# DLRM tower on one core: each gather waits for the last but one, in place of a wait behind each fifth

## What is computed

```python
e = jnp.stack([tbl_0[ids[:, 0]], ..., tbl_31[ids[:, 31]]], axis=1)   # (2048, 32, 16)
z = jnp.sum(e[:, row, :] * e[:, col, :], axis=2)                     # all pairs row < col: 496
h = jnp.concatenate([z, dense_ctx], axis=1)                          # 512 wide
h = jnp.maximum(h @ W_top1 + b_top1, 0.0)                            # 512 -> 512
h = jnp.maximum(h @ W_top2 + b_top2, 0.0)                            # 512 -> 256
y = h @ W_top3                                                       # 256 -> 1
```

## Time and profile before

| what | us |
|---|---|
| median of 3 runs | 389.74 |
| lowest and highest | 388.18 and 391.79 |
| span of the profiled execution, first to last instruction | 386.4 |
| around it, to the median | 3.3 |
| busy: TensorE's matmuls | 299.7 |
| busy: VectorE | 248.2 |
| busy: POOL | 228.5 |
| busy: ScalarE | 145.3 |

### The profile page before, as it was taken

One profiled execution on the slowest core, in us unless ns is written; L12 is line 12 of the kernel. 1 busy time (PEld: TensorE's weight loads), 2 busy tenths in 40 slices (PEclk: granted clock), 3 DMA queues, 4 the chain that ended last, 5 costly groups with the idle time before them and its releaser, 6 DMA issues.

```text
span 386.4 us, 7087 instructions
## 1 busy us (share of the span) xinstructions
PE 299.7 (78%) x2572; PEld 267.2 (69%) x2572; DVE 248.2 (64%) x326; ACT 145.3 (38%) x311; POOL 228.5 (59%) x250
## 2 busy tenths in 40 slices
PE   1767799886987967988676887877699786978477
PEld 1356689785887856877665886766598675867366
DVE  7699758675666666493756739464683955557541
ACT  3883543443162525244332424424243441113012
POOL 6456655566566656656665666566556656666700
PEclk9889779998999999989999998999969899899859
DMA  6670020202020202102020110202002000000000
GB/s 141 205 242 7 8 64 8 64 8 65 7 63 5 65 5 49 21 6 63 6 64 5 40 29 6 64 6 65 6 9 60 5 7 5 8 6 8 6 2 3
DMA packets 19036, 14.51 MB, mean 38 GB/s; under 512 B 9727, under 2 KB 16461, under 8 KB 19022
## 3 DMA queue, kind: packets, MB, share of 16 engines
q1 hardware_dynamic: 10284, 11.69, 9.5%
q0 software_dynamic: 7680, 1.98, 5.9%
q10 hardware_dynamic: 1058, 0.66, 0.6%
HBM read 14.24 MB, written 0.08 MB: 37 GB/s over the span
## 4 chain that ended last, share of the span: by engine, by line
issue 33%; POOL 28%; DMA 15%; PE 9%; DVE 6%; another core or an unknown queue 4%; ACT 3%; DVEq 1%; ACTq 0%; POOLq 0%
POOL emb L367 28%; DMA emb<-tbl,idx 15%; DVE emb L470 2%; PE bank L683 2%; DVE prod L489 2%; PE bank L663 2%; PE bank L692 1%; PE bank L645 1%; PE bank L780 1%; DVE prod L498 1%; ACT h1T L888 1%; ACT distance L844 1%; ACT onehot L854 1%; DMA idx<-ids 1%
## 5 line engine op out<-in xcount | busy, mean ns | idle before, releaser
L367 POOL DMA_INDIRECT emb<-tbl,idx x240 | 227.3, 947 | 138.4 <-DMA emb<-tbl,idx 73.4
L489 DVE TENSOR_TENSOR prod<-emb,bank 128x1904 f32<-128x1904 f32 (+5 forms) x51 | 94.5, 1854 | 88.3 <-DMA emb<-tbl,idx 88.3
L663 PE MATMUL bank<-ident,prod 128*128 128x128 f32 x768 | 102.8, 287 | 14.0 <-issue 8.6
L663 PEld LDWEIGHTS bank<-ident,prod 128*128 128x128 f32 x768 | 94.4, 197 | 15.9 <-issue 9.9
L683 PE MATMUL bank<-zT,w_sb 128*128 128x128 f32 x480 | 70.6, 295 | 13.6 <-ACT zT L882 12.9
L645 PE MATMUL bank<-parts,onehot 125*128 125x160 bf16 (+1 forms) x816 | 77.0, 244 | 1.4 <-issue 1.3
L683 PEld LDWEIGHTS bank<-zT,w_sb 128*128 128x128 f32 x480 | 63.6, 207 | 16.7 <-issue 14.9
L645 PEld LDWEIGHTS bank<-parts,onehot 125*128 125x128 bf16 x816 | 66.2, 106 | 12.3 <-issue 4.6
L470 DVE TENSOR_REDUCE emb<-bank 128x480 f32 (+5 forms) x96 | 52.7, 584 | 17.2 <-PE bank L645 8.8
L640 PE MATMUL bank<-far_ten,named_ten 100*128 100x480 bf16 (+1 forms) x64 | 24.8, 388 | 33.1 <-issue 24.5
L888 ACT ACTIVATE h1T<-bank,b_sb 128x128 f32<-128x128 f32 x60 | 21.5, 363 | 65.9 <-PE bank L683 26.5
(11 more groups left out here) (71 smaller groups left out, 126.5 us busy)
## 6 DMA issues: line engine op xcount, KB each, us to landing
gids<-small_ids_f SPq DMA_DIRECT2D x16, 544.0 KB
emb<-tbl,idx POOLq DMA_INDIRECT x240
w_sb<-w SPq DMA_DIRECT2D x1, 1024.0 KB
w_sb<-w SPq DMA_DIRECT2D x1, 512.0 KB
tab<-tbl SPq DMA_DIRECT2D x7, 56.0 KB
tab<-tbl SPq DMA_DIRECT2D x5, 70.0 KB
tab<-tbl ACTq DMA_DIRECT2D x5, 70.0 KB
z_last<-dense SPq DMA_DIRECT2D x16, 8.0 KB
```

The source lines that it names most:

```text
L367: nc.gpsimd.indirect_dma_start(emb[:, t, at:at + D], None, tables[f], bass.IndirectOffsetOnAxis(ap=idx[:, t, f:f + 1], axis=0)).then_inc(d ...
L489: return nc.vector.tensor_tensor(prod[:, at * D:(at + n * a) * D].rearrange("p (j i d) -> p j i d", j=n, d=D), strided(emb_at(t, PLACES[g] ...
L663: mm = nc.tensor.matmul(bank[:, Z_BANK + place, c * P:(c + 1) * P], v[:, d, :], ident[:], start=(d == 0), stop=(d == D - 1), is_transpose= ...
```

## The change

`RUN` and its waits go, and so do POOL's waits on `made`, the six semaphores `landed[g][..]` and the five `last_landed`. In their place stand two semaphores, `landed[0]` and `landed[1]`, which the gathers of the whole kernel use in turn, and each gather waits until the last but one has landed (`AHEAD = 2`). VectorE waits for a group, or for a piece of tile 15, by waiting for the last two gathers of it, one on each semaphore.

```diff
@@ constants
+L = len(LARGE)
...
-RUN = 5
+AHEAD = 2
@@ semaphores
-        landed = [[sem(f"landed{g}_{i}") for i in range(2)] for g in range(len(GROUPS))]
-        last_landed = [sem(f"last_landed{i}") for i in range(len(LAST_PIECES))]
+        landed = [sem(f"landed{i}") for i in range(AHEAD)]
@@ POOL
                 for g, n in enumerate(GROUPS):
-                    if t >= 2:
-
-                        pool.wait_ge(made, steps_done(t - 2, GROUP_STEPS[g]))
                     for i in range(n):
+                        gather = t * L + GROUP_AT[g] - S + i
+                        if gather >= AHEAD:
+
+                            pool.wait_ge(landed[gather % AHEAD], 16 * (gather // AHEAD))
                         f = FIELDS[GROUP_AT[g] + i]
                         at = (PLACES[g] + i) * D
-                        done = landed[g][t % 2]
-                        if t == LAST_TILE:
-                            for k, (group, first, count) in enumerate(LAST_PIECES):
-                                if group == g and first <= i < first + count:
-                                    done = last_landed[k]
                         nc.gpsimd.indirect_dma_start(
                             emb[:, t, at:at + D], None, tables[f],
                             bass.IndirectOffsetOnAxis(ap=idx[:, t, f:f + 1], axis=0)
-                        ).then_inc(done, 16)
-                        place = GROUP_AT[g] + i - S
-                        if t < LAST_TILE and place % RUN == RUN - 1:
-                            pool.wait_ge(done, 16 * (t // 2 * n + i + 1))
+                        ).then_inc(landed[gather % AHEAD], 16)
@@ VectorE
+            def wait_for_fields(place, lands, end):
+
+                for gather in range(place * L + end - S - AHEAD, place * L + end - S):
+                    dve.wait_ge(landed[gather % AHEAD],
+                                (lands - 1) * (2 * L // AHEAD * 16) + 16 * (gather // AHEAD + 1))
...
-                dve.wait_ge(landed[0][place], lands * 16 * GROUPS[0])
+                wait_for_fields(place, lands, GROUP_AT[1])
...
-                dve.wait_ge(landed[1][place], lands * 16 * GROUPS[1])
+                wait_for_fields(place, lands, GROUP_AT[2])
...
-                dve.wait_ge(landed[2][place], lands * 16 * GROUPS[2])
+                wait_for_fields(place, lands, GROUP_AT[3])
...
                 def piece(k):
                     g, first, n = LAST_PIECES[k]
-                    dve.wait_ge(last_landed[k], 16 * n)
+                    wait_for_fields(place, TILES // 2, GROUP_AT[g] + first + n)
                     return group_with_before(t, g, first, n)
```

More of the change, by code:

```diff
@@ L251, in dlrm_tower @@
         SMALL_STEP, GROUP0_STEP, CIRCLE0_STEP, GROUP1_STEP, CIRCLE1_STEP, BANK_STEP, LAST_STEP = range(7)
-        GROUP_STEPS = [GROUP0_STEP, GROUP1_STEP, BANK_STEP]
         STEPS = 7
```

## The result

The changed kernel took 586.43 us (median of 4 runs, 583.74 to 589.73) against 390.76 (4 runs, 388.18 to 392.63): ratio 1.502, 95% interval 1.493 to 1.511. My 349.3 us with the range 338 to 366 is wrong, and so is its sign. The profiled execution has a span of 584.4 us. In the experiments the same program, unaltered, took 365 to 371 us in each of 19 executions on four chips (on which chip the result was taken is not on record), so two things have to be explained, the 586 and the 368.

What follows compares the result with a forecast made beforehand. POOL's stream of gathers was taken as the bound: 3.0 + 23.3 + 15 x 19.3 + 14.3 = 330.1 us on POOL, span 343.6, taken as 346 for a possible stall, plus 3.3 around it: 349.3 us, range 338 to 366.

Steps and rivals of the forecast that it cites:

- so POOL stays the bound: Whole kernel: POOL's gathers, 19.3 to 20.4 us a tile, still set the pace, barely above TensorE's 18.9.
- 18.9 us: TensorE's tile without waits for fields: about 16.8 us of work plus a 2.09 us gap for ScalarE's copy of z.
- rival C: Unbroken gather stream starves TensorE: 7 us more for 15 gathers, 25.9 us a tile, time 435 us; chance 0.06.
- Waits behind each fifth gather gone, 2.57 a pair: POOL's gathers: without those waits each pair takes 2.57 us, 1.285 a gather, 19.3 us a tile.
- Each load costs one landing's delay, 13 x 1.1 = 14.3: POOL: each of 13 group-id loads in SyncE's loop delays one landing by 1.1 us; bounds 0 and 2 x 14.3.
- +4 us on tile 0: POOL's gathers beside the table and weight loads, 16 to 26 us: a pair takes 4.2 us, tile 0 23.3.
- Stall in tile 15, 2.4 us: TensorE's 16 matmuls in 9 us may recur in tile 15, ending the span at 347.5 not 343.6; 346 taken.
- Two waits for one on VectorE: 0: In front of each group VectorE waits on two semaphores; the last field decides as before, so no cost.
- removed waits on `made`: 0: POOL's waits for a step of tile t - 2: VectorE trails by less than a tile, so removal gains nothing.
- A: Rival: the engines bind, not POOL, at 20.25 us a tile; span 357.9, time 361 us; chance 0.28.
- B: Rival: POOL at its own 1.25 us a gather, loads hidden, engines bind at 18.9 a tile; 341 us; chance 0.14.
- D: Rival: landings with another gather in flight come 0.46 us later, a pair takes 3.03, time within 1% of 389.74; chance 0.05.

## Why the prediction was wrong

*The step that failed in the result: "so POOL stays the bound".* It rested on a TensorE that does its tile in 18.9 us whatever POOL does. In the execution of the result TensorE finished one product each 2.80 us while gathers ran, and tile 1 alone took 284.9 us on VectorE (66.20 to 351.13). I had the row that shows such a stall, and took it as a tail event worth 2.4 us; rival C took it as a state and gave it 0.06. C had the sign and the kind of rows ("matmuls stand apart by 0.7 us and more") right, its price of 7 us a tile far too low, and its mechanism was not borne out where it could be tried: four runs of kernels with a stream without pauses, ten executions in all, stand at 314.5 to 315.7 us. But none of them ran where the changed kernel was starved, so they do not refute it there. What starves TensorE is open. Shown is that the changed kernel did so in 4 of 4 executions in one place and in 0 of 19 in four series on four chips, that the kernel before had slight marks of it in that first place and none in the trace taken later, and that it lost 157 us in one of the 66 executions timed beside the experiments, at a granted clock that does not fit a starved TensorE (0.978 against 0.73). That the change made the kernel more prone to it in that place is what the result says; no run here could reproduce it, so no part of the change can be named for it, and no kernel here can be called safe from it. It is untested, too, what about the place matters (the chip, the moment), and whether the recording of the profile has a part in it.

*The steps that can be judged on the undisturbed runs (span 366.2, last gather at 353.8; forecast 343.6 to 346, and 328.8).*
- "Waits behind each fifth gather gone, 2.57 a pair": right in kind. Measured 1.303 us a gather, not 1.285: 3.4 us over tiles 2 to 15.
- "Each load costs one landing's delay, 13 x 1.1 = 14.3": mis-sized. Eleven loads cost 17.4 us, 1.6 each (two of my 13 fall in tiles 0 and 1); and eight late starts behind no fresh load, for which my sum had no term, cost 9.2: 6.0 beside blocks of the program's instructions, 3.2 by late restarts of POOL. Together 26.6, near my upper bound of 28.6, which I had set down to a different cause. They exceed my 14.3 by 12.3, half of the 25.0 us by which POOL was late.
- "+4 us on tile 0": tile 0 took 28.8 us and not 23.3, so 5.5 more; tile 1, which I put at 19.3, took 23.3, 4.0 more. Halfway between 2.57 and 5.75 was too low for a pair beside the tables.
- 5.5 + 4.0 + 3.4 + 12.3 = 25.2, against 25.0 measured.
- "Stall in tile 15, 2.4 us": it did not come. From the last gather to the end of the span are 12.3 us, where I had 17.2, of which 2.4 for the stall. The time around the span is 1.8 us and not 3.3.
- "Two waits for one on VectorE: 0" and "removed waits on `made`: 0": the trace gives no cost to the first. The second is wrong: putting them back costs 379.44 - 367.59 = 11.9 us on the same chip (one execution against six, which lie up to 3.7 us apart). Ahead of the first gather of groups 0 and 2 the median distance rises from 1.27 and 1.29 us to 1.75 and 1.85, some 0.5 us; ahead of group 1 it does not rise.

*The rivals.* A fell: tiles of 18.7 us were reached, and 16.03 behind the starvation, so the engines never bind at 20.25. My 18.9 for them was itself too high: it counted a gap of 2.09 us for the copy of z, and in the tiles of 16.03 us TensorE was busy for 16.03. B's stream at 1.25 us came true in the four runs with no limit or with five in flight (314.5 to 315.7 us, below B's 341, since the engines were faster too) and not for two in flight: at 2.6 against 2.50 a pair has no slack, and takes every late landing in full. The Trainium skill ("DMA: Bandwidth & Descriptors", section "Anatomy of one DMA — SWDGE (gpsimd) path") has a fixed cost of about 2 us. The trace with one in flight is somewhat above it: the landing comes 2.3 us after the gather's start (median), and the next gather starts 0.26 us behind the landing. That makes 2.6 us, more than the 2.50 of two gathers, and so two in flight are just too few. D fell: with another gather in flight a pair takes 2 x 1.303 = 2.61 us, not 3.03.

So undisturbed the change is worth 6% (ratios 0.935 to 0.941) and not 10.4, and leaves another 14% that five in flight give (368 to 315 us).

## What to carry to other kernels

Where an engine waits for the landing of its own transfers, count how many must be in flight by the worst landing and not by the usual one: here 1, 2, 3 and 5 in flight gave 658, 368, 326 and 315 us. A row in which an engine waits for nothing that is shown ("issue") inside a sequence with all inputs ready can be a sign about the place of the execution as much as about the kernel; run the same program again elsewhere before a theory is built on it. And where TensorE's rows look odd, count its products in program order against the releases of their readers. And let the first control of a series be the unaltered kernel: here it came twelfth, and all readings before it were without a base.

## What the runs showed of the hardware that was not expected

- TensorE can be held to one product in 2.80 us (one instruction in 1.40, distances in steps of 0.70) with its inputs ready and a DMA share of 0.09. It ended 14.4 us after the last gather was started. Its recorded starts were then up to 88 us ahead of the results.
- Without it the engines did a tile in 16.03 us with TensorE busy throughout, which no trace of the kernel before let one suppose.
- A gather's landing beside a load of 544 KB cost 1.6 us more, and beside a block of 8 to 16 KB of the program's own instructions 0.5 to 1.6 us. At two gathers (the ninth of tile 7, the first of tile 15) POOL restarted 1.6 us late; for the first of them the trace with one in flight shows the landing on time. The cause of that is open.
